# GpSimd takes the low halves of the FFN weights and the bias addition of the first chunk from VectorE

## What is computed

```python
q, k, v = split(x @ w_qkv)                 # 16 heads of 8
q, k = rope(rmsnorm(q) * q_scale), rope(rmsnorm(k) * k_scale)
attn = softmax(q @ k.T / sqrt(8)) @ v      # 2 sequences of 1024
x = layernorm(x + attn @ w_proj + b_proj)
h = silu(x @ w1 * s1) * (x @ w2 * s2)      # 128 -> 512
h = gelu(h @ h1 * t1)                      # 512 -> 512
h = gelu(h @ h2 * t2)                      # 512 -> 512
out = layernorm(x + h @ w3 * s3)           # 512 -> 128
```

## Time and profile before

| | |
|---|---|
| median of 3 runs | 375.9 us (373.97 to 377.68) |
| the profiled execution | 374.38 us, of which 372.7 is its span |
| TensorE matmul busy | 341.3 us, 92% |
| ScalarE busy | 304.7 us, 82% |
| VectorE busy | 221.7 us, 59% |
| GpSimd busy | 28.7 us, 8% |
| mean granted TensorE clock | 0.988 |

### The profile page before, as it was taken

The page is one execution under the profiler, slowest core; times in us unless marked ns, Lnnn a source line. Parts: engine busy times, 40 slices in busy tenths (PEclk is TensorE's granted clock), DMA queues, the critical chain, the costliest instruction groups (busy, mean ns, idle before and its releaser), DMA issues.

```text
span 372.7 us, 6253 instructions
## 1 busy us (share of the span) xinstructions
PE 341.3 (92%) x2091; PEld 135.8 (36%) x2091; DVE 221.7 (59%) x465; ACT 304.7 (82%) x350; POOL 28.7 (8%) x41
## 2 busy tenths in 40 slices
PE   7878999998999989999999999999999899999980
PEld 2412223222322353443222545333223534435850
DVE  1997988866547715364466453545477153667753
ACT  2689999899999898789999897989998987854330
POOL 2023111102100000001100000011000000011001
PEclk9989999999999999999999999999999999999997
DMA  7909464426202110111111200202021100000001
GB/s 222 293 31 346 159 211 165 168 82 244 86 21 99 38 67 2 60 42 59 70 59 41 87 13 4 96 0 105 25 98 36 64 0 0 0 29 0 2 0 33
DMA packets 12295, 29.42 MB, mean 79 GB/s; under 512 B 1138, under 2 KB 4082, under 8 KB 12274
## 3 DMA queue, kind: packets, MB, share of 16 engines
q1 hardware_dynamic: 8368, 16.23, 12.9%
q0 software_dynamic: 3328, 12.06, 9.1%
q10 hardware_dynamic: 578, 0.85, 0.8%
HBM read 17.64 MB, written 9.44 MB: 73 GB/s over the span
## 4 chain that ended last, share of the span: by engine, by line
PE 63%; DVE 14%; ACT 10%; DMA 6%; issue 5%; POOL 1%; SPq 0%; POOLq 0%; DVEq 0%; ACTq 0%
PE ps L508 23%; PE ps L555 15%; PE ps L494 11%; ACT probs L843 8%; PE ps L545 4%; PE ps L663 4%; DMA va<-v_all 4%; DVE ffn L1060 2%; PE ps L461 2%; PE ps L625 2%; DMA xT<-in_x_t 1%; DMA k_scr<-parts 1%; DVE r L941 1%; PE ps L697 1%; PE ps L525 1%
## 5 line engine op out<-in xcount | busy, mean ns | idle before, releaser
L843 ACT ACTIVATE probs<-ps 128x1024 f32<-128x1024 f32 x256 | 242.6, 1035 | 24.8 <-PE ps L494 24.5
L508 PE MATMUL ps<-probs,va 128*9 128x512 f32 x896 | 112.7, 594 | 3.7 <-ACT probs L843 2.7
L494 PE MATMUL ps<-qa,ka 32*128 32x512 f32 x512 | 77.0, 499 | 8.2 <-ACT probs L843 6.0
L494 PEld LDWEIGHTS ps<-qa,ka 32*128 32x128 f32 x512 | 31.7, 183 | 105.6 <-ACT probs L843 60.3
L1060 DVE TENSOR_SCALAR ffn<-ps,col 128x512 f32<-128x512 f32 x36 | 27.0, 751 | 55.0 <-PE ps L555 50.8
L555 PE MATMUL ps<-g_hi,w_hi 128*128 128x512 f32 x108 | 45.5, 421 | 1.7 <-DVE ffn L1060 1.2
L555 PE MATMUL ps<-g_lo,w_hi 128*128 128x512 f32 x108 | 42.5, 393 | 0.0
L508 PEld LDWEIGHTS ps<-probs,va 128*9 128x9 f32 x896 | 15.8, 89 | 48.9 <-issue 27.3
L1035 DVE TENSOR_TENSOR g_lo<-ffn,g_hi 128x512 fp32r<-128x512 f32 x36 | 24.9, 692 | 1.2
L555 PEld LDWEIGHTS ps<-g_hi,w_hi 128*128 128x128 f32 x108 | 20.3, 188 | 14.5 <-DVE g_lo L1035 4.0
L439 POOL TENSOR_TENSOR rs<-ve,mhalf 128x4 f32<-128x4 f32 x6 | 6.1, 1022 | 227.5 <-DVE ve L1023 227.5
(11 more groups left out here) (129 smaller groups left out, 322.3 us busy)
## 6 DMA issues: line engine op xcount, KB each, us to landing
ka<-k_scr SPq DMA_DIRECT2D x14, 512.0 KB
k_scr<-parts POOLq DMA_DIRECT2D x8, 512.0 KB, 4.4
q_scr<-parts POOLq DMA_DIRECT2D x8, 512.0 KB, 5.1
qa<-q_scr SPq DMA_DIRECT2D x14, 256.0 KB
va<-v_all SPq DMA_DIRECT2D x14, 144.0 KB
ffn<-in_h POOLq DMA_DIRECT2D x1, 1024.0 KB, 6.1
h_raw<-in_h POOLq DMA_DIRECT2D x1, 1024.0 KB, 8.7
xT<-in_x_t SPq DMA_DIRECT2D x3, 256.0 KB, 6.6
```

The lines of the kernel that those rows point to most:

```text
L494: mm = pe.matmul(s_tile(u)[:, i, :], ka[rows, slot, kt * P:(kt + 1) * P], qa[rows, slot, :], start=True, stop=not shifted)
L508: mm = pe.matmul(ps[32 * h:32 * h + VW, O_BANK, :], v, probs[:, step % 4, h, :], start=(kt == 0), stop=(kt == KT - 1))
L843: nc.scalar.activation(probs[:, step % 4, 2 * pair:2 * pair + 2, :], s_tile(u), ACT.Exp).then_inc(exp_done, 1)
```

## The change

VectorE keeps the high halves, now without a wait between them (`high_part`, `w_high`). GpSimd makes the low halves (`low_part`, `low_half`), each when its high half is there, and counts them in `w_low`; VectorE waits for that count before it takes a largest value. GpSimd also adds the bias, between the first and the second half of h2, and VectorE waits for `bias_added` before chunk 1. GpSimd loads w1, w2 and w3 after its own two subtractions for h1; the store of task 0's rows (`store(3, 1, 1)`) comes after the bias. VectorE makes the high half of w3 directly behind that of w1 and w2, ahead of `turn_group(2)`.

```diff
@@ -231,7 +231,9 @@
         v_evac = sem("v_evac")
         k_out = [sem(f"k_out{t}") for t in range(NCH)]
         q_out = [sem(f"q_out{t}") for t in range(NCH)]
-        h1_taken = sem("h1_stage_taken")
+        w_high = sem("w_high_written")
+        w_low = sem("w_low_written")
+        bias_added = sem("bias_added")
         aug_in = [sem("aug_in0"), sem("aug_in1")]
         shift_in = [sem("shift_in0"), sem("shift_in1")]
         qk_ready = sem("qk_ready")
@@ -417,19 +419,36 @@
                     pool.dma_start((rows[:, i, :, :], rows[:, :, i, :])[at],
                                  parts_of(t, at)[:, i:i + 1, :].bitcast(F32).to_broadcast([P, PARTS, CH])).then_inc((k_out, q_out)[at][t], 16)
 
+            def low_part(raw, at, n, turn):
+
+                pool.wait_ge(w_high, turn)
+                pool.tensor_tensor(w_lo[:, at:at + n], raw, w_hi[:, at:at + n].bitcast(F32), ALU.subtract).then_inc(w_low, 1)
+
+            def low_half(raw, at, i, turn):
+                half = HM * HID // 2
+                low_part(raw[:, i * half:(i + 1) * half], at + i * half, half, turn)
+
             pool.wait_ge(qk_proj, 4)
             stage(h1_raw, h1, HM, in_h1)
             store(0, 0, 0)
             store(1, 0, 1)
             stage(h2_raw, h2, HM, in_h2)
             store(2, 1, 0)
-            pool.wait_ge(h1_taken, 1)
+            low_half(h1_raw, H1, 0, 1)
+            low_half(h1_raw, H1, 1, 2)
+            pool.wait_ge(w_low, 2)
             stage(w_raw[:, W1:W1 + HID], w1, 1, in_w123)
             stage(w_raw[:, W2:W2 + HID], w2, 1, in_w123)
             stage(w_raw[:, 2 * HID:2 * HID + HM * P], w3, HM, in_w123)
+            low_half(h2_raw, H2, 0, 3)
+            pool.wait_ge(in_res, 64)
+            pool.tensor_tensor(xb[:], xb[:], bias_b[:, None, :].to_broadcast([P, NCH * TILES, P]), ALU.add).then_inc(bias_added, 1)
             store(3, 1, 1)
+            low_half(h2_raw, H2, 1, 4)
             store(4, 2, 0)
             store(5, 2, 1)
+            low_part(w_raw[:, 0:2 * HID], W1, 2 * HID, 5)
+            low_part(w_raw[:, 2 * HID:2 * HID + HM * P], W3, HM * P, 6)
             store(6, 3, 0)
             store(7, 3, 1)
 
@@ -1158,11 +1177,8 @@
 
             w_max = stats[:].rearrange("p t s -> p (t s)")
 
-            def split_weights(raw, at, n):
-
-                hi = w_hi[:, at:at + n]
-                link(nc.vector.tensor_copy(hi, raw), 0)
-                return nc.vector.tensor_tensor(w_lo[:, at:at + n], raw, hi.bitcast(F32), ALU.subtract)
+            def high_part(raw, at, n):
+                nc.vector.tensor_copy(w_hi[:, at:at + n], raw).then_inc(w_high, 1)
 
             def largest_low(i, at, n):
                 return nc.vector.tensor_reduce(w_max[:, i:i + 1], w_lo[:, at:at + n].bitcast(F32), AX.X, ALU.max, apply_absolute_value=True)
@@ -1175,45 +1191,46 @@
 
                 half = HM * HID // 2
 
-                def split_half(raw, at, i):
-                    return split_weights(raw[:, i * half:(i + 1) * half], at + i * half, half)
+                def high_half(raw, at, i):
+                    high_part(raw[:, i * half:(i + 1) * half], at + i * half, half)
 
                 late_products(0)
                 turn_group(0)
                 late_swap(0)
                 dve.wait_ge(in_h1, 16)
-                split_half(h1_raw, H1, 0)
-                split_half(h1_raw, H1, 1).then_inc(h1_taken, 1)
+                high_half(h1_raw, H1, 0)
+                high_half(h1_raw, H1, 1)
                 dve.wait_ge(in_h2, 16)
-                split_half(h2_raw, H2, 0)
+                high_half(h2_raw, H2, 0)
                 late_products(1)
-                dve.wait_ge(in_res, 64)
-                link(nc.vector.tensor_tensor(xb[:], xb[:], bias_b[:, None, :].to_broadcast([P, NCH * TILES, P]), ALU.add), 0)
                 late_swap(1)
                 late_sum(0)
                 late_rows(0)
-                link(split_half(h2_raw, H2, 1), 0)
+                high_half(h2_raw, H2, 1)
                 late_products(2)
                 turn_group(1)
                 late_swap(2)
                 late_sum(1)
                 late_rows(1)
-                dve.wait_ge(h1_taken, 1)
+                dve.wait_ge(w_low, 2)
                 largest_low(0, H1, HM * HID)
                 late_sum(2)
                 late_v(2)
                 late_rows(2)
                 late_products(3)
+                dve.wait_ge(w_low, 4)
                 largest_low(1, H2, HM * HID)
                 late_swap(3)
                 dve.wait_ge(in_w123, 48)
-                split_weights(w_raw[:, 0:2 * HID], W1, 2 * HID)
+                high_part(w_raw[:, 0:2 * HID], W1, 2 * HID)
+                high_part(w_raw[:, 2 * HID:2 * HID + HM * P], W3, HM * P)
                 turn_group(2)
-                link(split_weights(w_raw[:, 2 * HID:2 * HID + HM * P], W3, HM * P), 0)
                 late_products(4)
                 late_sum(3)
                 late_swap(4)
+                dve.wait_ge(w_low, 5)
                 largest_low(2, W1, 2 * HID)
+                dve.wait_ge(w_low, 6)
                 link(largest_low(3, W3, HM * P), 0)
                 nc.vector.tensor_reduce(ve[:, 0:1], w_max[:, 0:4], AX.X, ALU.max).then_inc(w_split, 1)
                 late_rows(3)
@@ -1273,6 +1290,7 @@
                 with dve.Fori(NG, NG * NCH) as n:
                     row_maxima(n)
             start = links[0]
+            dve.wait_ge(bias_added, 1)
             with dve.Fori(1, NCH) as c:
                 use[0], links[0] = 0, 0
                 chunk(c, MIX_CHUNK * (c - 1) + MIX_FIRST, CHAIN_CHUNK * (c - 1) + start)
```

## The result

The changed kernel takes 378.4 us (median of 20 runs, 376.9 to 380.9), the kernel before 376.6 us in the same comparison; the ratio is 1.0063 with a 95% interval of 1.0037 to 1.0088. The ratio is that of the means of the fast runs, those within 1.5% of the fastest of their kernel; by it the changed kernel is 2.4 us slower (by the medians 1.8), which is inside the 1% that was called no change. The profiled execution took 380.2 us with a span of 378.2.

What follows compares the result with a forecast made beforehand. TensorE and ScalarE were taken as the full engines, VectorE not. VectorE's relief counted 0 and the delayed exponential +2.0 us: 376.4 us from the profiled execution, 377.9 on the median; 8-in-10 range 374.3 to 381.0.

Steps and rivals of the forecast that it cites:

- VectorE's relief is worth nothing: First chunk: 9.1 us taken from VectorE give 0, since ScalarE and TensorE do not wait for it there.
- The prices: GpSimd's operations in the first chunk: 2.2 us per subtraction of 1024 elements, 4.0 us for the bias.
- The estimate of two passes: GpSimd reads its two inputs one after the other; one pass would give 1.3 us per subtraction, three 3.1.
- The hold: Wide GpSimd and VectorE operations in the first chunk: whichever began first holds the other until finished.
- the upper end: Of the range from no hindrance (0) to a whole wait between VectorE and GpSimd, the whole wait was taken.
- Rival A: First chunk: sharing without whole waits, or subtractions under 1.8 us; nothing on the path, 375.4 to 375.9 us; chance 0.25.
- rival B: GpSimd needs three passes, 3.1 us per subtraction and 5.8 for the bias; exponential +5.5, 381.4 us; chance 0.14.
- The schedule: First chunk: task 0's sum ends at 50.85, bias holds VectorE to 54.85, parts at 56.75, exponential +2.0 us.
- the forecast formula: Time of VectorE's parts for ScalarE's square: 46.15 plus three subtractions plus the bias addition, on GpSimd.
- The loads and the store of GpSimd's queue at no cost: Weight loads 2.5 us later, task 0's store about 5.5 us later; both wanted much later, so 0.
- Rival C: TensorE, starved for 2 us, loses its granted clock; about 1.5 us on top of 2.0, 379.4 us; chance 0.05.

Runs made afterwards that it cites:

- relief_only: Changed kernel with low halves zero-filled by GpSimd at the start, no subtractions and no bias addition; 376.6 us, ratio 1.0101 to the kernel before.
- bias_late: Changed kernel with only the bias addition moved on GpSimd, behind the store of task 2's rows; 375.2 us, ratio 0.999 to the kernel before.
- reordered: Changed kernel with h2's first low half ahead of the weight loads and the bias behind task 2's store; 373.8 us, 0.9901 of the kernel before.
- before_loads_late: Kernel before with one edit: loads of w1, w2 and w3 behind the store of task 0's rows; 373.6 us, ratio 0.9903.
- fill_place: Changed kernel with two write-only 128x2048 fills in the bias's place and the bias behind task 2's store; 375.5 us in one execution.
- bias_half: Changed kernel with the bias split: 8 of 16 tiles in the old place, 8 behind task 2's store; 375.4 us, 0.995 of the kernel before.
- bias_only: Kernel before with only the bias addition moved to GpSimd, behind the weight loads, low halves left on VectorE; 377.0 us, ratio 1.0046.
- lows_only: Changed kernel with low halves on GpSimd but the bias back at its old place on VectorE; 375.5 us, 1.0012 of the kernel before.
- after_again: The changed kernel unedited, run again for a second profile; 378.8 us, ratio 1.0081 to the kernel before.

## Why the prediction was right, step by step

**VectorE's relief is worth nothing.** Right. It is carried by `relief_only`, `bias_late` and the equality of `reordered` with `before_loads_late` (0.9901 and 0.9903).

**The prices.** A subtraction was put at 2.2 us and measured 2.36 to 2.46 where nothing held it, the bias at 4.0 and measured 4.55, 9 and 14% more. The estimate of two passes came close; whether GpSimd does make two passes no run shows. The figure of the Trainium skill, GPSIMD Engine Reference, § 3 "Performance versus the Vector engine", 4.5 us for 2048 elements, agrees with the trace; it was the better price.

**The hold.** Right: the upper end that was taken, a whole wait, is what the rows show, for two inputs against GpSimd's reads (6.57 us), for a cast (2.86 us), and with GpSimd as the one held (2.83 in place of 2.4). The Trainium skill, SBUF — State Buffer, § "Who interferes with whom", has a VectorE instruction with two SBUF inputs collide with GpSimd's reads but not with its writes, fast casts collide with both, and whichever began first hold the other for its whole length. The runs agree in all of this. Rival A, sharing without whole waits, is refuted by the same rows, and rival B by the prices.

**The schedule.** One step was wrong: that VectorE's sum would get in between the subtraction and the bias at 50.15. It is held through both (6.57 us). The same was assumed for the cast between h1's two subtractions, and there it held: what one operation does in this place does not carry over to the other. This changes little, because the sum has to be done before or after the addition: the forecast formula gives 46.15 + 3 x 2.39 + 4.55 = 57.9 with the measured prices, and 57.2 without the sum's 0.7 us in the middle; the parts came at 57.45 + 0.69 - 0.88 = 57.3 on the clock of the profile before. The place (task 0's late rows, ScalarE's square of task 2) was right, and the delay of the exponential was 2.45 us where 2.0 were forecast.

**The loads and the store of GpSimd's queue at no cost.** The store: right. The loads: mis-sized. Their place was priced at 0 to 0.5 us by the one wait of the profile; moved behind the store in the kernel before they are worth 1.0% (0.57 to 1.37). In the changed kernel they go out 2.5 us later, as forecast (46.86 - 0.88 against 43.51), but what that could have given lies under the wait of the square: TensorE's wait for group 2 is 0.28 and 0.54 us in the two profiles, against 0.79.

**Rival C, the clock.** It was given 0.05 and happened in both profiles of the changed kernel: in the first the clock fell near 58, while TensorE idled 2.66 us for the exponentials (to 59.80), in the second near 62, after it had idled 2.38 us (to 60.45). In `bias_late` and `fill_place` there was no such idle and no fall near there. It was priced at 1.5 us more; ScalarE's second idle time grew by 2.4 us in the first profile and by 1.2 in the second (2.69 and 1.47 against 0.31). The changed kernel is nevertheless only 2.4 us over the one before, about the wait alone. Both its profiles are of executions above its medians (380.2 and 382.3 against 378.4 and 378.8 us), and the one of the kernel before is below its own. That the total met the forecast so closely, without the fall in the sum, is in part luck. The kernel before has falls of its own in many of its runs: over its 23 runs in the last comparison the mean granted clock goes from 0.989 to 0.972 and the time from 372.9 to 381.8 us, with a correlation of -0.74. So part of what the fall costs the changed kernel the other one pays too.

**Open.** What late loads give, and why. The ratio says 3.7 us, the profiles 0.5 us of wait. Part of the 3.7 may be the chip: the kernel before took longer on it (mean 376.7 us) than on the other two (375.2 and 375.6), and `bias_half`, whose loads go out early and whose square waits 0.75 us, was 0.5% under it as well; against `bias_half` the late loads are worth 1.5 us in `reordered` and 1.9 in `before_loads_late` (means). The profiled executions do not show the gain: 375.3 us for `reordered` and 374.8 for `before_loads_late`, against 374.4 for the kernel before, whose clock of 0.988 is near the top of its runs.

TensorE's wait for group 2 differs from profile to profile, from 0.28 to 1.89 us over the kernels with early loads, so the 0.79 of the profile before need not be typical. After the waits of 1.43 and 1.89 us (`relief_only`, `bias_half`) the clock fell and ScalarE idled 1.89 us more a few us later; after the shorter ones, up to 1.12 in `bias_only`, and one of 1.62 in `lows_only`, it did not. A wait of that size with its fall comes to about 3.5 us, and the mean clock of the runs (0.982 in `reordered` and `before_loads_late`, 0.978 before, same chip) points that way. How often the kernel before runs so, its one profile does not show.

There is a second such place. Near the end of the chunk TensorE idles 1.2 us in every one of the 14 profiles, and in 8 of them the clock is at half for some us from there or at most 2 us later on, in kernels of every kind; it is not in the profiles of the kernel before and the changed kernel, but is in `after_again`, `reordered` and `before_loads_late`. In `reordered` it costs 0.9 us between the table load and the long row of exponentials in chunk 1 (101.41 - 91.58 against 100.58 - 91.67). Like the fall near 58, it was not priced by an experiment of its own, apart from the wait ahead of it.

## What to carry to other kernels

Before elementwise work goes from VectorE to GpSimd, look not at busy shares but at what VectorE does at that moment: two-input operations and casts in SBUF stand still while GpSimd reads, and do not always get in between two of its operations, so a 0.7 us operation can take the sum of all that stands there. Put such work where VectorE has reads from PSUM, reductions or nothing to do, never two pieces in a row ahead of a deadline. And when work moves in a queue that also issues transfers, the transfers move with it: ask which load each of them will meet, and take the price from repeated times, since one profile of each kernel did not show it here.

## What the runs showed of the hardware

- GpSimd, 128 partitions in fp32: a subtraction of 1024 elements 2.36 to 2.46 us, of 2048 elements with a broadcast input 4.55 to 4.69, an addition with the same tile as both inputs 3.62, a fill of 2048 elements 1.81. VectorE needs 1.23 and 2.28 us for the first two.
- VectorE's two-input sum of 0.69 us waited for two and for three GpSimd operations that read and followed each other without idle time (6.57, 10.10 us); a cast got in between two such subtractions (2.86 us) but not between two fills (2.45 us for 0.43). A two-input product kept its 0.69 us beside a fill. A product from PSUM with one SBUF input, the reductions and the transposes out of PSUM kept their 0.75, 2.28 and 0.71 us beside GpSimd's subtractions and additions.
- GpSimd in turn waits for a running two-input operation of VectorE (2.83 us in place of 2.4) and for a cast (5.52 us for h1's two subtractions).
